# Strassen's scheme for the neighbour sums of two graph layers

## What is computed

```
def _gcn_layer(x, row, col, norm, W, b, n):
    h = x @ W
    msg = h[row] * norm[:, None]
    out = jax.ops.segment_sum(msg, col, num_segments=n)
    return out + b
...
h = relu(_gcn_layer(h, row, col, norm, W1, b1, n))
h = relu(_gcn_layer(h, row, col, norm, W2, b2, n))
h = _gcn_layer(h, row, col, norm, W3, b3, n)
```

## Time and profile before

| | us |
|---|---|
| median of 3 runs (1399.9 to 1404.13) | 1401.78 |
| span of the profiled execution | 1400.5 |
| PE busy | 1363.9 |
| DVE busy | 886.7 |
| ACT busy | 568.6 |
| POOL busy | 88.0 |
| products, layers 0, 1, 2, 3 | 45.5, 42.9, 42.9, 50.6 |
| sums, layers 0, 1, 2, 3 | 112.6, 112.6, 121.8, 117.6 |

### The profile page before, as it was taken

How to read it: one execution, slowest core, us unless ns; L and a number is a source line. 1 busy time by engine, 2 the same in 40 slices (tenths; PEclk the granted TensorE clock), 3 DMA queues, 4 the chain that set the end, 5 groups by cost and what they waited for, 6 DMA issues and landing times.

```text
span 1400.5 us, 26694 instructions
## 1 busy us (share of the span) xinstructions
PE 1363.9 (97%) x11285; PEld 843.1 (60%) x11285; DVE 886.7 (63%) x1381; ACT 568.6 (41%) x980; POOL 88.0 (6%) x86
## 2 busy tenths in 40 slices
PE   9889999989998999999999999999999999999998
PEld 8779898989996655544444444454444445344443
DVE  7998998999988886567555666542354223532323
ACT  2666566656554457411142113221253224422312
POOL 3120010101002110000001000011100000000000
PEclk9999999999999999999999999999999999999999
DMA  9634344335348723000002000022210222563201
GB/s 335 227 114 148 137 138 137 126 119 177 120 146 286 238 94 108 1 31 1 0 0 61 0 0 1 1 59 77 68 40 29 73 71 78 200 212 104 91 0 60
DMA packets 71333, 136.92 MB, mean 98 GB/s; under 512 B 11908, under 2 KB 24324, under 8 KB 69798
## 3 DMA queue, kind: packets, MB, share of 16 engines
q1 hardware_dynamic: 68542, 123.98, 26.8%
q0 software_dynamic: 1280, 5.77, 1.5%
q10 hardware_dynamic: 1384, 5.38, 1.1%
HBM read 81.79 MB, written 53.32 MB: 96 GB/s over the span
## 4 chain that ended last, share of the span: by engine, by line
PE 83%; DVE 11%; ACT 2%; issue 2%; DMA 1%; POOL 0%; ACTq 0%; SPq 0%; DVEq 0%; POOLq 0%
PE banks L2305 31%; PE banks L2239 13%; PE banks L2369 12%; PE banks L1255 6%; PE banks L1655 4%; DVE x_sb L894 3%; PE banks L1192 3%; PE banks L1209 2%; PE banks L1266 2%; PE banks L1166 2%; DVE x_sb L877 1%; PE banks L2183 1%; PE banks L1625 1%; PE banks L298 1%; PE banks L1643 1%
## 5 line engine op out<-in xcount | busy, mean ns | idle before, releaser
L2305 PE MATMUL banks<-g,count 128*128 128x512 f16 x1024 | 227.6, 379 | 0.5 <-DVE tiles L2571 0.5
L2305 PE MATMUL banks<-count,g 128*128 128x512 f16 x1024 | 223.6, 379 | 0.0
L2239 PE MATMUL banks<-w_parts,h_parts 128*128 128x512 f16 x960 | 215.3, 379 | 1.7 <-DVE g L2520 1.4
L2305 PEld LDWEIGHTS banks<-count,g 128*128 128x128 f16 x1024 | 99.6, 98 | 118.0
L2305 PEld LDWEIGHTS banks<-g,count 128*128 128x128 f16 x1024 | 99.7, 98 | 113.6 <-DVE tiles L2571 1.0
L2369 PE MATMUL banks<-g,part 128*128 128x512 f16 x768 | 165.9, 379 | 0.0
L2239 PEld LDWEIGHTS banks<-w_parts,h_parts 128*128 128x128 f16 x960 | 91.2, 98 | 115.4 <-issue 11.4
L894 DVE TENSOR_TENSOR x_sb<-eb_parts,x_sb 128x4096 f16<-128x4096 f16 x64 | 146.0, 2281 | 0.0
L1255 PE MATMUL banks<-x_sb 128*128 128x128 f16 x2048 | 126.9, 221 | 11.9 <-DVE x_sb L894 11.8
L1255 PEld LDWEIGHTS banks<-x_sb 128*128 128x128 f16 x2048 | 120.9, 99 | 15.3 <-DVE x_sb L894 14.2
L2369 PEld LDWEIGHTS banks<-g,part 128*128 128x128 f16 x768 | 75.1, 98 | 90.6
(11 more groups left out here) (346 smaller groups left out, 1902.5 us busy)
## 6 DMA issues: line engine op xcount, KB each, us to landing
weight_dram<-w_new SPq DMA_DIRECT2D x60, 256.0 KB, 2.6
count<-weight_dram SPq DMA_DIRECT2D x29, 512.0 KB, 7.1
qk_dram<-stage SPq DMA_DIRECT2D x64, 128.0 KB, 2.6
tiles<-x_dram SPq DMA_DIRECT2D x32, 256.0 KB, 3.5
x_dram<-tiles SPq DMA_DIRECT2D x32, 256.0 KB, 2.8
count<-in_x SPq DMA_DIRECT2D x4, 1024.0 KB, 12.8
h<-in_x SPq DMA_DIRECT2D x16, 256.0 KB, 4.3
h_dram<-h_t SPq DMA_DIRECT2D x8, 512.0 KB, 3.3
```

The lines of the kernel that those rows point to most:

```text
L2239: mm = pe.matmul(out, m.h_parts[:, slot, zh, k], m.w_parts[:, zw, k], start=n == 0 and layer != 3, stop=n == len(passes) - 1)
L2305: mm = pe.matmul(m.agg_ps[:, b], lhs, rhs, start=i == 0 and z == 0, stop=i == NT - 1 and z == 1)
```

## The change

For layers 0 and 1 the sum is seen as a product of two matrices, each cut in four blocks: the values by halves of the features and of the source nodes, the counts by halves of the source nodes and of the destinations. Eight products of blocks become seven, by Strassen's scheme, on sums and differences of blocks. A destination half is done as two chunk pairs `h` = 0 and 1 (chunks `h` and `h` + 2), each with seven steps of 32 matmuls; a step fills or adds to two banks.

- `paired_sums` replaces `sums` for layers 0 and 1 on all engines. Each step needs a combination of values (A11, A12, A22 as they are; S1, S2, S3, S4 combined) and of counts (chunks as they are, or T1 to T4 in the new buffer `mix`).
- In the products of these layers ACT no longer makes the high part of a tile: it writes the scaled f32 result into `h_t`. High parts are made later by `operand_hi` (ACT) and low parts by `operand_lo` (DVE), in pieces of four tiles and 256 features; `combine` (DVE) makes the combinations in place. Half of them (q = 1) can only be made once the last tile is there.
- The counts are combined by DVE (`mix_one` to `mix_four`), each piece when PE has read the piece before it.
- Banks that hold a product used twice are copied out by ACT (`keep_single`) and added later by DVE (`join`) and POOL.
- DVE's `sum_out` is gone: ACT does the row sums (`row_sum`, 32 pieces with an accumulator), and DVE the maxima (`count_peak`), now in layer 2, one for each finished tile. `edge_scale` moves from layer 2 to layer 3.
- `h_scale` becomes `pair_peak` and `pair_scale`, once for each `h`.
- The ring of banks in layers 1 and 2 has five places, and evictions come four tiles late.
- Loads of the third bias and of the first three raw tiles come later in SP's queue; the loop additions come earlier in layer 0.

Cut to its core, in the order of ACT (`product_hi`, `paired_sums`), PE (the steps) and DVE (`operands`, the branch of `paired_sums` for h = 1, `finish`):

```diff
 def slots(layer):
-    return 3 if layer in (1, 2) else 2
+    return 5 if layer in (1, 2) else 2
...
+HIGHS_AFTER = {3: [("A11", 0)], 7: [("A11", 1)], 11: [("A22", 0), ("A12", 0)], 12: [("S1", 0), ("S3", 0)], 13: [("S2", 0)], 14: [("S4", 0)],
+               15: [("A22", 1), ("A12", 1), ("S1", 1), ("S3", 1), ("S2", 1), ("S4", 1)]}
...
     def product_hi(layer, t):
...
+        if layer < 2:
+            act.activation(m.h_t[:, :, t * P:(t + 1) * P], prod_bank(m, layer, t).rearrange("p (k n) -> p k n", k=KT), ACT.Copy,
+                           scale=scale).then_inc(s["ghi"], 1)
+            for name, q in HIGHS_AFTER.get(t, ()):
+                operand_hi(layer, name, q)
+            return
...
+    def paired_sums(layer):
+        for h in range(PAIRS):
+            keep_single(layer, h, 1, nodes(m, h, 2))
+            keep_single(layer, h, 2, nodes(m, h + 2, 2))
+            for t in rows[0:2]:
+                row_sum(t)
+            keep_single(layer, h, 4, nodes(m, h + 2, 0))
+            if h == 0:
+                for k in range(KT):
+                    weight_hi(layer + 1, k)
...
+            act.wait_ge(s["fin"], 4 * number + 1)
+            relu_sums(layer, h, (0, 1))
+            for t in rows[2:4]:
+                row_sum(t)
+            if h == 1:
+                split_hi(layer + 1, 0)
+                split_hi(layer + 1, 1)
...
+            if layer == 1 and h == 0:
+                pe.wait_ge(s["ghi"], NT * layer + NT - 1)
+            step(1, one, "A11", lambda i: m.count[:, i, h], True)
+            step(2, other, "S1", lambda i: m.mix[:, i], True, mixed("T1", 2))
+            pe.wait_ge(s["kept"], 3 * pair + 1)
+            step(3, one, "A12", lambda i: m.count[:, HT + i, h], False)
+            pe.wait_ge(s["kept"], 3 * pair + 2)
+            step(4, other, "S4", lambda i: m.count[:, HT + i, 2 + h], False)
+            pe.wait_ge(s["fin"], 4 * pair + 1)
+            step(5, one, "S3", lambda i: m.mix[:, i], True, mixed("T3", 2))
+            pe.wait_ge(s["kept"], 3 * pair + 3)
+            step(6, other, "S2", lambda i: m.mix[:, i], True, mixed("T2", 4))
+            pe.wait_ge(s["joined"], 4 * pair + 1)
+            step(7, one, "A22", lambda i: m.mix[:, i], False, mixed("T4", 4))
...
+    def operands(layer, t):
+        if t == 11:
+            operand_lo(layer, "A22", 0)
+            combine(layer, "S1", 0)
+            operand_lo(layer, "A12", 0)
+            combine(layer, "S3", 0)
+        if t == 12:
+            operand_lo(layer, "S1", 0)
+            combine(layer, "S2", 0)
...
+            else:
+                mix_one(layer, h, 0)
+                mix_one(layer, h, 1)
+                pair_peak(layer + 1, 0)
...
+                first_sum(layer, h)
+                split_lo(layer + 1, 0)
+                split_lo(layer + 1, 1)
+            largest(0, nodes(m, h, 0), AX.XY, relu_mark(layer, h, "C11"))
+            for part in range(4):
+                mix_two(layer, h, part)
...
                 settle(dve.bn_stats(m.stats[:, 6 * b:6 * b + 6], m.tiles[:, b]))
+                if layer == 2:
+                    count_peak(t)
                 op = dve.bn_aggr(m.moments[:, b], m.stats[:, 6 * b:6 * b + 6])
```

More of the change, by code:

```diff
@@ L2016, in split_hi @@
         if layer in (1, 2):
-            act.activation(out, source, ACT.Copy, scale=m.h_scale[:, layer - 1, c:c + 1]).then_inc(s["hi"], 1)
+            act.activation(out, source, ACT.Copy, scale=m.h_scale[:, layer - 1, c % 2:c % 2 + 1]).then_inc(s["hi"], 1)
         else:
@@ L2147, in layers_act @@
         products(layer)
-        sums(layer)
+        if layer < 2:
+            paired_sums(layer)
+        else:
+            sums(layer)
     products(4)
@@ L2286, in sums, with beside @@
+    def beside(layer, h, number, i):
+        if (number, i) == ((3, 6) if h == 0 else (3, 2)):
+            peak_row()
+        if (number, i) == ((4, 4) if h == 0 else (4, 2)):
+            peak_all()
     def sums(layer):
@@ new lines, in mix_one, with mix_three @@
+    def mix_one(layer, h, part):
+        tiles = slice(PER * part, PER * (part + 1))
+        before = PAIRS * layer + h - 1
+        if before >= 0:
+            dve.wait_ge(s["agg"], step_mark(before // 2, before % 2, STEPS) + before % 2)
+        dve.tensor_tensor(m.mix[:, tiles], m.count[:, tiles, 2 + h], m.count[:, tiles, h], ALU.subtract).then_inc(s["mixed"], 1)
+    def mix_three(layer, h, part):
+        tiles = slice(PER * part, PER * (part + 1))
+        if part == 0:
+            dve.wait_ge(s["mix_used"], used_mark(layer, h, 2, 1))
+        else:
+            dve.wait_ge(s["agg"], step_mark(layer, h, 2))
+        dve.tensor_tensor(m.mix[:, tiles], m.count[:, HT + PER * part:HT + PER * (part + 1), 2 + h], m.count[:, tiles, 2 + h],
+                          ALU.subtract).then_inc(s["mixed"], 1)
@@ new lines, in await_used, with mix_two @@
+    def await_used(layer, h, step, part):
+        if part < 3:
+            dve.wait_ge(s["mix_used"], used_mark(layer, h, step, part))
+        else:
+            dve.wait_ge(s["agg"], step_mark(layer, h, step))
+    def mix_two(layer, h, part):
+        tiles = slice(2 * part, 2 * part + 2)
+        await_used(layer, h, 5, part)
+        dve.wait_ge(s["mixed"], mix_mark(layer, h, "T3", part // 2))
+        dve.tensor_tensor(m.mix[:, tiles], m.mix[:, tiles], m.count[:, tiles, h], ALU.add).then_inc(s["mixed"], 1)
@@ L2686, in late_semaphores @@
     attended = dict(zip(attention, cleared))
-    over = cleared[len(attention):] + later
+    over = cleared[len(attention):] + later + [keep.first[n] for n in PROJECT_SEMS.split()]
     table = dict(zip(layers, over))
```

410 lines of the change are left out of this document (309 added, 101 removed).

## The result

The changed kernel takes 1426.8 us (median of 4 runs, 1423.4 to 1428.5) against 1402.7 for the kernel before it on the same chip (4 runs): a ratio of 1.0173, 95% interval 1.0153 to 1.0194. It is slower by 24 us. The forecast was 1416, with a range of 1404 to 1427: the sign and the range held, the size was 10 us short. The time lies 0.2 us inside the upper end of the range, so that it lies inside at all is luck.

A forecast was written before the change was run, and what follows sets the result against it. TensorE was taken as the bound, busy 1363.9 of 1400.5 us. Waits of 37.4 plus clock loss of 6.1 made 43.5, less 29.3 removed: net +14.2 on the median 1401.78, so 1416, range 1404 to 1427.

The forecast's parts named there:

- Removed work: Sums of layers 0 and 1: 448 matmuls instead of 512 each, 27.7 us, plus 1.6 for peak matmuls; 29.3 saved.
- Products of layer 0: End of layer 0's products: DVE operations ahead of the splits delay product 14 by 3.8 and make product 15 4.4 late.
- clock: After five longer PE waits the clock falls to half: 1.7 us at three, 1.0 at product 14; 6.1 in all.
- step 3's wait: Third step of the sums waits for kept results: 1.6 us in layer 0, 2.5 in layer 1.
- Step 6: Sixth step of each half, layers 0 and 1, waits for a mix: 1.1 and 5.2 us, 6.3 a layer.
- Layer 1, 6.9 and 2.5: Start of layer 1's sums: step 1 waits 6.9 us for product 14's eviction, step 3 then 2.5.
- Layer 2's turn: Layer 2's first turn: four count maxima, 2.25 us each net, stall PE 7.4 us.
- Prices: Costs taken for added operations: DVE combination 1.25 with its wait, ACT high part 1.15, kept copy 1.7, row sum 1.15.
- The rival with heavier kept copies and row sums (D): Kept copies at 2.2 and row sums at 2.28 us give 1428; chance 0.1.
- Between the layers: Two transitions after layers 0 and 1: DVE's work delays product 2, POOL's passes hidden; 1.0 us each.
- Products of layer 3: Edge scale moves to layer 3, its first tile still finished 4 us before PE wants its bank: 0.

The follow-up runs named there:

- experiment 8: Changed kernel with reordered products, splits, high parts, kept copy and count maxima, and GpSimd's two C22 passes moved to DVE: 1379.2 us, 0.985 of the kernel before.
- experiment 5: Changed kernel with layer 0's splits of products 14 and 15 ahead of some DVE operations, ACT's high parts of S1 to S4 a product later: 1430.3 us.
- Experiment 2: Changed kernel with ACT making the next layer's first two high parts ahead of the last two row sums, in second halves of both layers: 1412.6 us.
- experiment 3: Changed kernel with ACT evicting products 12 to 14 of layer 1 ahead of the copies of S1 to S4: 1426.2 us.
- experiment 4: Changed kernel with GpSimd's two passes over C22 in each half cut to one column of each block: 1420.1 us.
- experiment 6: Changed kernel with splits for products 2 and 3 ahead of the maxima and last relus in the transitions to layers 1 and 2: 1421.8 us.

## Why the forecast was right, and where it was short

The forecast was right in its sign and, but for one term, in its account of where PE waits; what it had at 1.0 us for each transition between the layers was nearly 6.

- **Removed work, 29.3.** Right: the sums nearly without waits measure 98.2 and 98.9 (experiment 8).
- **Products of layer 0, 4.4 and 1.0 of clock.** Right in sum (5.6 measured). Product 14 waited 3.02, the clock cost 1.4, and 1.2 us came earlier, in the products before it, which wasn't foreseen. Of the latter 0.9 lies at one turn (0.56 of wait for ACT, and the turn itself 1.36 in place of 1.04). But the wait had no full price, as the prediction half said ("its delay also eats into step 3's wait"): experiment 5.
- **Step 6, 6.3 a layer.** Right: 0.86 and 4.86, with 2.0 (layer 0) and 1.7 (layer 1) of clock where 1.7 was taken. Experiment 2 shows that the cause is ACT's order, as worked out.
- **Layer 1, 6.9 and 2.5.** 6.57 and 0.41, and 2.3 of half clock that the prediction said step 3's wait would take up. 9.4 forecast for step 1 to 3, 9.3 measured. Right in sum, but each as a price of its own is wrong: experiment 3. Its working for step 3 has DVE through 12 more operations of 1.25 at 20.4 where 5.0 + 15.0 is 20.0, which changes nothing.
- **Layer 2's turn, 7.4 and 1.7.** 6.9 and 1.8. Right.
- **Prices.** A combination 1.23, a high part 1.04 (taken: 1.15), the kept copy 1.94 (1.7; the bounds were 1.15 and 2.2), a row sum piece 1.04 and 0.19 for its accumulator (1.15), a relu of 512 0.80. The rival with heavier kept copies and row sums (D) gave 1428, nearer to the time than the forecast, for a wrong reason: a row sum took 1.23 with its accumulator, not 2.28.
- **Between the layers, 1.0 each. This term failed:** 5.8 and 6.0, so 9.8 of the 11.5 us by which the span of 1426.2 missed the forecast's 1414.7. The step was "POOL's two passes (1.27 for 512, so 2.5 each) start 4 us before the end and feed a relu that DVE needs 3 us after it: hidden by 0.5, else they add what they exceed". It asked only when POOL's result is there, and not what the pass does to DVE's own work meanwhile: 2.0 us on one multiplication and 1.1 on the next. For that reason the first join and multiplication of C21, which the sum left out as done before the last step ends, came behind it. With the passes taken away the first transition measures 12.7 in place of 17.0 (experiment 4): of these 4.3 us 2.8 are PE's wait (1.42 in place of 4.26, the 3.1 of DVE's two operations less 0.3) and 1.4 are the half clock behind it, which the forecast had counted at other waits and not here. The rest of the term was right: 1.5 for product 2's wait without POOL, 1.42 measured.
- **Products of layer 3, 0.** 0.9: the last group's count maxima delay a split there by 1.1 us. Small, and missed.
- **Start of the kernel, +2.2.** Scatter between executions.

## What to carry to other kernels

Of several waits at one place only the last chain has a price: before a wait is priced, ask when the slowest queue behind it is through, and start that queue earlier rather than clear the wait in front. The fewer matmuls of such a scheme are worth their full time only if the work that feeds them is laid beside the stage before; here the places of a few splits and of four count maxima and the order of the tiles decided between 1.7% slower and 1.5% faster, with the same busy time on DVE and ACT to 2 us. A helper on GpSimd is not free cover when DVE works on two SBUF operands at the time: here it was worth nothing (1381.4 against 1379.2 without it).

## What the runs showed of the hardware

**DVE and GpSimd stop each other.** With a GpSimd pass in work, a DVE operation with two operands in SBUF stood still until the pass ended (3.25 against 1.22, 1.76 against 0.69, 1.50 against 0.75), and one with an operand in a bank did not (1.06 beside the pass, 1.05 without). It goes the other way too: the passes themselves took 3.38 and 3.22 us where the prediction had 2.5, each having begun while a DVE operation with two SBUF operands was in work, and cut down to two elements in experiment 4 they still took 1.24 and 1.18, as long as the DVE operations that had begun just before them (1.23 and 1.22). The Trainium skill says this (SBUF — State Buffer, "Who interferes with whom"): a DVE instruction with two SBUF inputs contends with a GpSimd instruction that reads SBUF, and who comes second is blocked for the whole instruction. The trace agrees in each of these rows. With the two excesses of these rows (2.0 and 1.1), known only afterwards, the term for a transition would have been an estimated 4 us in place of 1, before any loss of clock.

**Half clock after a wait does not follow from the wait alone.** In the changed kernel PE waited 3.02 us before product 14 of layer 0, and the granted clock then fell to half; with layer 0's splits moved it waited 3.05 us before step 3, 1.43 shortly ahead of it, and the clock stayed full. Stretches of the changed kernel (the wait, after it) and of experiment 5 (before the wait, the wait, after it):

```profile
582.90:586.00 3.10, 0.09 (x2) 0.04 (x2) 3.03 (x4) 1.88 (x3) 0.00 (x0) 0.91 0.00 0
586.00:589.00 3.00, 3.00 (x8) 1.07 (x9) 2.93 (x4) 2.03 (x4) 0.00 (x0) 0.53 0.00 0
```

```profile
601.20:604.80 3.60, 3.56 (x16) 1.49 (x16) 3.52 (x3) 1.05 (x1) 0.00 (x0) 1.00 0.00 0
604.80:607.90 3.10, 0.07 (x1) 0.00 (x0) 3.00 (x4) 2.90 (x3) 0.00 (x0) 1.00 0.01 3
607.90:611.00 3.10, 3.09 (x15) 1.44 (x16) 3.10 (x3) 3.07 (x4) 0.00 (x0) 1.00 0.03 5
```

In experiment 6 the same waits, 0.70 and 1.48 us before product 4, stand in both transitions; behind them the clock stayed full in layer 1 and fell in layer 2:

```profile
712.80:716.00 3.20, 3.20 (x15) 1.48 (x16) 0.75 (x1) 1.30 (x2) 0.00 (x0) 1.00 0.00 0
...
873.65:877.00 3.35, 3.35 (x10) 1.26 (x11) 2.02 (x3) 1.30 (x2) 0.00 (x0) 0.64 0.00 0
```

Every wait of 4.3 to 6.9 us of the kernels above, in the stages compared here, did end in half clock, and it cost 1.3 to 3.1 us. What decides for waits of 3 us or less stays open.
